# Last attention: four of twelve score tiles are clipped after the exponential, by GpSimd, and the lower bound becomes a constant

## The chip, the core and the metric

One NeuronCore of one Trainium2 chip runs the whole program as one launch. The metric is the device time of an execution in microseconds; several executions are timed and the median is given. One execution was also recorded by the hardware profiler; all rows below are from it. Engines: PE is TensorE, DVE is VectorE, ACT is ScalarE, POOL is GpSimd, SP is the queue that issues most transfers.

## The reference

Four layers, each a cross attention and a feed-forward part, on x of 32 batches x 56 tokens x 128 features, with a context of 1500 keys x 96 features for each batch. The change touches only the attention of the last layer:

```python
# B = 32, Nq = 56, Nkv = 1500, H = 16 heads of D = 8, scale = 8 ** -0.5
q = (query @ Wq + bq)      # query = layernorm(x)
k = (key_value @ Wk + bk)  # key_value = ctx_768
v = (key_value @ Wv + bv)
attn = einsum("bhqd,bhkd->bhqk", q, k) * scale
attn = clip(attn, -10000.0, 10000.0)
attn = softmax(attn, axis=-1)
attn = where(any(isnan(attn)), 1.0 / Nkv, attn)
x = x + tanh(g_xattn[3]) * (einsum("bhqk,bhkd->bhqd", attn, v) as [B, Nq, 128] @ Wo + bo)
```

## The kernel before

`clipped_pass` (line 1617) is the last attention. Each batch b has 12 key tiles of 125 keys (KT = 12, KP = 125). A score tile is 125 keys x 896, the 896 being 16 heads x 56 queries, and takes two PSUM banks of 448 columns; two such pairs (`SB`) alternate. P holds three tiles of weights in SBUF.

Keys and queries go into the tensor engine in bf16 as three parts each, and six products of parts (`NPROD`) are stacked on 96 partitions. The parts of the keys are made by `copy_keys` and `second_of_keys` on ScalarE and `rest_of_keys` (line 1846) and `third_of_keys` (line 1851) on GpSimd, three pieces of 500 columns each, and placed into the stacked tile KS by six transfers of SP (`place_keys`, line 1792). The parts of the queries are placed into QS by twelve transfers that GpSimd issues (`place_queries`, line 1769). Both run three batches ahead (b + 3), in a ring of four tiles.

The softmax needs the maximum of each row of scores before its exponentials. So each batch is scored twice. In the maximum pass 12 chunks of 112 queries x 1000 keys (`chunks`, line 1994, two matmuls) go through one pair of PSUM banks (6 and 7), and VectorE reduces each (`chunk_max`, line 2232). After the twelfth, the maximum is clipped (line 2240), GpSimd splits its negative into three bf16 parts (`max_parts`, line 1858), TensorE turns these (lines 1934 and 1935), ScalarE copies them (2128, 2129), and SP writes them as three more rows of the stacked queries, against rows of ones in the keys. The scores of the second pass thus come out with the maximum already subtracted. The same chain makes a row of lower bounds, -clip - max, which SP stores to memory and broadcasts to 125 partitions (`LB`, lines 1797 and 1801).

In the second pass each tile n goes through `score` (PE, line 2014, 8 matmuls), `clip_tile` (DVE, line 2249, from PSUM to P: min with 0, max with LB), the exponential (ACT, line 2188, in place in P), and `weigh` (PE, line 2027, 16 matmuls with the values, a column of ones giving the sum).

Every engine has its order written out by hand, in steps k = 0 to 11 of batch b. TensorE in step k: `score` of tile k + 2, `weigh` of tile k, the chunk of the maximum pass (for b + 1 if k < 3, chunks 9 to 11; else for b + 2, chunk k - 3), and at most one thing in the fifth bank (`MISC`): keys of b + 3 in k = 0, 1, 2; in k = 3 the sums of a pair of batches (even b) or the projection (odd b); the turn of the maximum of b + 1 in k = 4; the spread of the sums in k = 5 (even b); values of b + 1 in k = 7 to 10. VectorE in step k: clip of tile k + 2, maximum of that step's chunk. ScalarE before the exponential of tile n empties the fifth bank's content of step n - 3, and at n = 6, 7, 8 makes the second key parts. GpSimd in batch b: the twelve query transfers of b + 3, the key rest of piece 0, the parts of the maximum of b + 1, the rests of pieces 1 and 2, the three third parts, in even batches the norm of the pair before (lines 1882 and 1884), and in the first two batches the rows of ones (line 1743). An instruction waits for the semaphores of what it reads and of who used its buffer before; what stands behind it on its engine waits too.

Of the kernel before, what the change touches and what calls it, by code (L numbers as in the profile page):

```python
# [13 lines left out]
F32 = mybir.dt.float32  # L14
# [14 lines left out]
TT = 112  # L29
# [1556 lines left out]
class Eight(Batch):  # L1586
# [6 lines left out]

CLIP_SIGNALS = ["w_in", "q_made", "q_scaled", "q_split", "q_first", "q_zeroed", "keys_zeroed", "sums_zeroed", "ones_set",
# [5 lines left out]
                "max_in0", "max_in1", "lb_out", "lb_in0", "lb_in1", "scored", "clipped", "exped", "weighed",  # L1600
# [16 lines left out]
def clipped_pass(core, L, S, src, bo, scale, clip, csum, ctx, norm):  # L1617
# [3 lines left out]
    def sb(n, shape, dt=F32, c=ctx):  # L1621
        return core.sb(f"{L}_{n}", shape, dt, c)
# [14 lines left out]
    zero, most = sb("zero", [TT, 8]), sb("most", [TT, 8])  # L1637
    nm, r1, ST = sb("nm", [TT, 8]), sb("r1", [TT, 8]), sb("st", [TT, 32])
# [3 lines left out]
    MT, LBT = sb("mt", [24, TT], BF16), sb("lbt", [8, TT])  # L1642
    low = [nc.dram_tensor(f"{L}_low{s}", (1, HQ), F32).ap() for s in range(2)]
# [11 lines left out]
    def two(ap):  # L1655
        return ap.rearrange("p (a n) -> p a n", a=2)
# [12 lines left out]
    def chunk_of(b, k):  # L1669

        return (b + 1, 9 + k) if k < 3 else (b + 2, k - 3)

# [67 lines left out]
    def ones_in_keys(pool, n):  # L1740
        nc.gpsimd.memset(KS[n][0:96, PAIRS * NK:].bitcast(F32), 0.0).then_inc(S["keys_zeroed"], 1)
        pool.wait_ge(S["keys_zeroed"], 2 * n + 1)
        nc.gpsimd.memset(KS[n][96:128, :].bitcast(F32), TWO_ONES).then_inc(S["keys_zeroed"], 1)
        pool.wait_ge(S["keys_zeroed"], 2 * n + 2)
# [32 lines left out]
    with nc.Block() as block:  # L1777
        @block.sync
        def _(sp):
# [50 lines left out]
        def _(pool):  # L1830
            link = core.linker(pool, "pool")
            link(nc.gpsimd.memset(zero[:, :], 0.0))
            link(nc.gpsimd.memset(most[:, :], clip))
            link(nc.gpsimd.memset(ok[:, :], 0.0))

            def place_queries(b):
# [4 lines left out]
                place_products(pool, b, 0, range(NPROD), f"q_in{b.r % 4}")  # L1841
                place_products(pool, b, 1, range(0 if b.r else 3, NPROD), f"q_in{b.r % 4}")
# [11 lines left out]
            def max_parts(b):  # L1854
                done = S["parts"]

                def op(out, a, c, how):
                    nc.gpsimd.tensor_tensor(out, a, c, how).then_inc(done, 1)
                pool.wait_ge(S["max_ready"], b.lin(1, 1))
                op(nm[:, :], zero[:, :], mc[:, :], ALU.subtract)  # L1860
                op(b0[:, :], zero[:, :], mc[:, :], ALU.subtract)
                pool.wait_ge(done, b.lin(8, 2))
# [3 lines left out]
                pool.wait_ge(done, b.lin(8, 5))  # L1866
                op(b1[:, :], r1[:, :], zero[:, :], ALU.add)
                pool.wait_ge(done, b.lin(8, 6))
                op(ST[:, 8:16], b1[:, :], zero[:, :], ALU.add)
                op(ST[:, 16:24], r1[:, :], b1[:, :], ALU.subtract)  # L1870
# [45 lines left out]
        def _(pe):  # L1916
# [89 lines left out]
            def score(b, n):  # L2006
                if n == 0:
                    pe.wait_ge(S["keys_zeroed"], min(2 * b.r + 2, 8))
# [10 lines left out]
            def weigh(b, j):  # L2019
                pe.wait_ge(S["exped"], b.lin(12, j + 1))  # L2020
# [76 lines left out]
        def _(act):  # L2097
# [76 lines left out]
            def body(b):  # L2174
                for n in range(KT):
# [11 lines left out]
                    act.wait_ge(S["clipped"], b.lin(12, n + 1))  # L2187
                    nc.scalar.activation(two(P[0:KP, n % 3, :]), two(P[0:KP, n % 3, :]), ACT.Exp  # L2188
                                         ).then_inc(S["exped"], 1)
# [25 lines left out]
        def _(dve):  # L2215
# [14 lines left out]
            def chunk_max(b, c, pair=0):  # L2230
# [21 lines left out]

            def b_uses(b):
                if b.turn is None:
                    return (b.r // 2 + 1) * 16
                return 64 * b.turn + (b.r // 2 + 1) * 16
# [1521 lines left out]
```

## Time and profile before

| | |
|---|---|
| median of 3 runs | 4267.36 us (4258.15 to 4271.67) |
| profiled execution | 4270.6 us, its span 4269.0 us |
| DVE / PE / ACT / POOL busy, share of the span | 60 / 86 / 48 / 34 % |
| last attention, second passes | from 3368 to 4199 us of the span |
| transfers, mean over the span | 102 GB/s |

The profile lists each engine's busy time, groups of instructions with the idle time before them and who ended it, and instructions in order of time. "L2249" is line 2249 of the kernel. "x8" is a count, and a duration of a merged row runs from the first start to the last end. "idle before <- X" is the time that the engine stood still until X released it. Durations of matmuls include their way through the array, so neighbours overlap; differences of starts tell what a group really takes of the engine.

### The profile page before, as it was taken

The page shows a single profiled execution, that of the slowest core. Times are in us where ns is not written, and L with a number is a line of the kernel's source. Part 1 is how long each engine was busy: PE and PEld are TensorE (multiplying, and loading weights), DVE is VectorE, ACT ScalarE, POOL GpSimd, SP SyncE. Part 2 cuts the span into 40 slices and gives each one's busy share as a digit, 9 for nine tenths or more (in the row PEclk, how much of TensorE's full clock was granted, in tenths as well). Part 3 has the DMA queues.
Part 4 walks back from the last instruction along what each step waited for, and adds up shares of the span by engine and source line. Part 5 has one row for each costly group of instructions (what it writes and reads, how often), then busy time and mean ns, then how long its engine had stood idle before and what let it go on. Part 6 is the DMA issues. An engine that isn't in the chain of part 4 may idle for free. (4 is left out here: it accounts for less than half of the span.)

```text
span 4269.0 us, 84337 instructions
## 1 busy us (share of the span) xinstructions
PE 3663.6 (86%) x33162; PEld 2471.7 (58%) x33162; DVE 2581.8 (60%) x3504; ACT 2050.0 (48%) x2961; POOL 1434.1 (34%) x1893
## 2 busy tenths in 40 slices
PE   7499999936279999998999998669958799999997
PEld 7367777723146666664666666347733366666664
DVE  8556666553244455424555542457644799999995
ACT  7277777701014434442444343146522477777764
POOL 0265555122422323212322320012201666665540
PEclk9699999958669999997999998879969799999998
DMA  6277777445132323212333321011000666666650
GB/s 170 56 163 179 172 172 178 119 167 217 33 80 70 85 80 93 78 49 67 88 85 86 84 81 36 9 57 46 16 18 16 133 156 152 152 155 156 156 134 24
DMA packets 197789, 434.35 MB, mean 102 GB/s; under 512 B 46364, under 2 KB 99638, under 8 KB 197341
## 3 DMA queue, kind: packets, MB, share of 16 engines
q1 hardware_dynamic: 122636, 339.40, 30.7%
q0 software_dynamic: 39328, 47.04, 5.1%
q10 hardware_dynamic: 35504, 43.39, 3.7%
q8 instruction: 231, 3.78, 0.4%
q14 instruction: 90, 0.73, 0.1%
HBM read 244.66 MB, written 32.67 MB: 65 GB/s over the span
## 5 line engine op out<-in xcount | busy, mean ns | idle before, releaser
L1501 DVE TENSOR_REDUCE L_mp<-ps 128x2 f32<-128x1000 f32 (+1 forms) x352 | 403.3, 1151 | 555.3 <-PE ps L1320 551.9
L1483 ACT ACTIVATE L_p<-ps 125x896 f32<-125x896 f32 x384 | 352.2, 917 | 607.6 <-PE ps L1345 536.1
L1357 PE MATMUL ps<-L_p,L_cn 125*97 125x448 f32 x1536 | 639.3, 538 | 0.0
L2188 ACT ACTIVATE L_p<-L_p 125x896 f32<-125x896 f32 x384 | 364.5, 950 | 226.7 <-DVE L_p L2249 222.8
L2232 DVE TENSOR_REDUCE L_mp<-ps 112x2 f32<-112x1000 f32 x384 | 454.7, 1188 | 18.9 <-PE ps L1994 18.8
L2249 DVE SCALAR_TENSOR_TENSOR L_p<-ps,xn 125x896 f32<-125x896 f32 x384 | 413.5, 1079 | 17.1 <-PE ps L2014 16.8
L1343 PE MATMUL ps<-L_qh,L_ch 97*125 97x448 f32 x768 | 385.9, 502 | 14.5 <-DMA L_qh<-L_mc 14.5
L1357 PEld LDWEIGHTS ps<-L_p,L_cn 125*97 125x97 f32 x1536 | 250.4, 163 | 199.9 <-issue 165.9
L1994 PE MATMUL ps<-L_ks,L_qs 96*128 96x500 bf16 x768 | 236.7, 393 | 78.3 <-DVE L_mp L2232 65.5
L1344 PE MATMUL ps<-L_ql,L_ch 96*125 96x448 f32 x768 | 284.0, 370 | 0.0
L1345 PE MATMUL ps<-L_qh,L_cl 96*125 96x448 f32 x768 | 282.5, 368 | 0.0
L938 ACT ACTIVATE L_p<-ps,rk 125x896 f32<-125x896 f32 x256 | 257.6, 1007 | 51.0 <-PE ps L794 46.8
L1320 PE MATMUL ps<-L_cr,L_qb 96*128 96x500 f32 x672 | 242.8, 445 | 14.1 <-DVE L_mp L1501 8.1
L1769 POOL DMA_DIRECT2D L_qs<-L_q_part x381 | 211.9, 564 | 99.5 <-PE ps L2014 92.9
L2014 PEld LDWEIGHTS ps<-L_qs,L_ks 128*128 128x128 bf16 x3072 | 189.2, 98 | 75.0 <-issue 45.7
L794 PEld LDWEIGHTS ps<-L_qs,L_ks 128*128 128x128 bf16 x3072 | 188.1, 98 | 72.9 <-issue 54.8
L2027 PE MATMUL ps<-L_p,L_vs 125*18 125x112 f32 x6144 | 223.1, 263 | 3.4 <-ACT L_p L2188 2.9
L794 PE MATMUL ps<-L_qs,L_ks 128*128 128x112 bf16 x3072 | 216.1, 213 | 3.4 <-ACT L_p L938 3.4
L720 POOL DMA_DIRECT2D L_qs<-L_q_part x384 | 214.5, 567 | 7.6 <-DVEq L1060 6.8
L2014 PE MATMUL ps<-L_qs,L_ks 128*128 128x112 bf16 x3072 | 215.4, 213 | 1.7 <-DVE L_p L2249 1.0
L963 DVE COPY L_vs<-ps 125x384 f32<-125x384 f32 x128 | 70.9, 554 | 232.1 <-PE ps L770 232.0
L1272 POOL TENSOR_TENSOR L_un<-L_ue,L_rb 96x896 f32<-96x896 f32 x32 | 67.1, 2095 | 424.5 <-DMA L_rb<-L_den 424.5
(541 smaller groups left out, 7328.9 us busy)
## 6 DMA issues: line engine op xcount, KB each, us to landing
L_ks<-L_k_part SPq DMA_DIRECT2D x288, 375.0 KB, 6.0
L_ks<-L_k_first SPq DMA_DIRECT2D x96, 375.0 KB
moe_w<-in_L_w SPq DMA_DIRECT2D x64, 512.0 KB
L_cn<-in_ctxN SPq DMA_DIRECT2D x32, 568.4 KB
cs_ct<-in_ctxT SPq DMA_DIRECT2D x32, 562.5 KB, 4.2
L_raw<-in_ctxT SPq DMA_DIRECT2D x32, 562.5 KB, 5.0
L_cr<-in_ctxT POOLq DMA_DIRECT2D x32, 562.5 KB, 5.0
L_ch<-in_ctxT POOLq DMA_DIRECT2D x32, 562.5 KB, 4.5
```

Source lines behind the costliest of these rows:

```text
L794: mm = nc.tensor.matmul(SB[n % 2][:, m // 4, m % 4 * 2 * NQ:(m % 4 + 1) * 2 * NQ] .rearrange("p (j q) -> p j q", j=2), KS[b.r % 3][:, k0:k ...
L938: nc.scalar.activation(weights_at[n % 3][0:KP, :].rearrange("p (a n) -> p a n", a=2), SB[n % 2][0:KP], ACT.Exp, scale=rk[:, b.lin(KT, n):b ...
L1343: nc.tensor.matmul(SB[n % 2][:, a, :], CH[s][:, k], QH[s][:, q], start=True, stop=False)
L1344: nc.tensor.matmul(SB[n % 2][:, a, :], CH[s][0:DC, k], QL[s][:, q], start=False, stop=False)
L1345: mm = nc.tensor.matmul(SB[n % 2][:, a, :], CL[s][:, k], QH[s][0:DC, q], start=False, stop=True)
L1357: mm = nc.tensor.matmul(U[:, a, :], CN[s][:, j, :], P[:, n % 2, a * HALF:(a + 1) * HALF], start=(j == 0), stop=(j == KT - 1))
L1483: nc.scalar.activation(two(P[:, n % 2, :]), SB[n % 2], ACT.Exp).then_inc(S["exped"].sem, 1)
L1501: nc.vector.tensor_reduce(mp[:, 2 * k:2 * k + n], ps[:, bank:bank + n, 0:500], AX.X, ALU.max).then_inc(S["chunk_maxed"].sem, 1)
L2014: mm = nc.tensor.matmul(SB[n % 2][:, m // 4, m % 4 * 2 * NQ:(m % 4 + 1) * 2 * NQ] .rearrange("p (j q) -> p j q", j=2), KS[b.r % 4][:, k0:k ...
L2188: nc.scalar.activation(two(P[0:KP, n % 3, :]), two(P[0:KP, n % 3, :]), ACT.Exp).then_inc(S["exped"], 1)
L2232: nc.vector.tensor_reduce(mp[:, 2 * c:2 * c + 2], ps[0:TT, CB[pair], 0:500], AX.X, ALU.max).then_inc(S["chunk_maxed"], 1)
L2249: nc.vector.scalar_tensor_tensor(out=two(P[0:KP, n % 3, :]), in0=SB[n % 2][0:KP], scalar=0.0, in1=two(LB[0:KP, b.r % 2, :]), op0=ALU.min, ...
```

## The change

Tiles 2, 6, 8 and 11 of each batch (`FLOORED`) are no longer clipped by VectorE. ScalarE takes their exponential straight from PSUM into P, and GpSimd then bounds the weights in P in place, min with 1 and max with exp(-64). Their PSUM pair is free when the exponential is done, their weights are ready when GpSimd is done. The other eight tiles are clipped by VectorE with two constants, 0 and -64, in place of the row. The row of lower bounds, its subtraction, transpose, copy, store and broadcast are gone; the maximum is clipped to [64 - clip, clip]. The order of GpSimd changes: the four bounds stand among its other work, and the twelve query transfers are spread in three groups of four. The rows of ones are filled in halves.

```diff
+RANGE = 64.0
+LEAST = float(np.exp(-RANGE))
+    FLOORED = (2, 6, 8, 11)
+    CLIPPED = [n for n in range(KT) if n not in FLOORED]
+    def bank_read(b, n):
+        if n in FLOORED:
+            return S["exped"], b.lin(12, n + 1)
+        return S["clipped"], b.lin(8, CLIPPED.index(n) + 1)
+    def weights_ready(b, n):
+        if n in FLOORED:
+            return S["floored"], b.lin(4, FLOORED.index(n) + 1)
+        return S["exped"], b.lin(12, n + 1)
...
             def place_max(b):
                 sp.wait_ge(S["turn_copied"], b.lin(1, 1))
-                sp.dma_start(low[b.r % 2].rearrange("o (t n) -> (o t) n", t=8), LBT[:, :]).then_inc(S["lb_out"], 16)
                 sp.dma_start(QS[b.r % 4][96:99, 0:HQ].rearrange("r (m n) -> r m n", n=2 * NQ), MT[:, :]
                              ).then_inc(S[f"max_in{b.r % 2}"], 16)
-                sp.wait_ge(S["lb_out"], b.lin(16, 16))
-                sp.dma_start(LB[0:KP, b.r % 2, :], low[b.r % 2].to_broadcast([KP, HQ])
-                             ).then_inc(S[f"lb_in{b.r % 2}"], 16)
...
-                op(ST[:, 24:32], nm[:, :], most[:, :], ALU.subtract)
...
+            def floor_tile(b, n):
+                pool.wait_ge(S["exped"], b.lin(12, n + 1))
+                nc.gpsimd.tensor_scalar(P[0:KP, n % 3, :], P[0:KP, n % 3, :], 1.0, LEAST, ALU.min, ALU.max
+                                        ).then_inc(S["floored"], 1)
+
             def body(b):
-                if (b + 3).there():
-                    place_queries(b + 3)
-                if (b + 3).there():
+                keys = (b + 3).there()
+                floor_tile(b, 2)
+                if keys:
+                    place_queries(b + 3, range(0, 2))
                     rest_of_keys(b + 3, 0)
                 if (b + 1).there():
                     max_parts(b + 1)
-                if (b + 3).there():
-                    for c in (1, 2):
-                        rest_of_keys(b + 3, c)
-                    for c in range(3):
-                        third_of_keys(b + 3, c)
+                if keys:
+                    rest_of_keys(b + 3, 1)
+                floor_tile(b, 6)
+                if keys:
+                    rest_of_keys(b + 3, 2)
+                    third_of_keys(b + 3, 0)
+                floor_tile(b, 8)
+                if keys:
+                    third_of_keys(b + 3, 1)
+                    third_of_keys(b + 3, 2)
+                    place_queries(b + 3, range(2, 4))
+                if b.r < 2:
+                    nc.gpsimd.memset(KS[b.r + 2][0:96, PAIRS * NK:].bitcast(F32), 0.0).then_inc(S["keys_zeroed"], 1)
+                    pool.wait_ge(S["keys_zeroed"], 3 * (b.r + 2) + 1)
+                    ones_row_part(pool, b.r + 2, 0)
+                floor_tile(b, 11)
                 if b.r % 2 == 0 and (b - 2).there():
                     norm(b - 2)
+                if keys:
+                    place_queries(b + 3, range(4, NPROD))
                 if b.r < 2:
-                    pool.wait_ge(S["keys_third"], (b + 3).lin(3, 3))
-                    ones_in_keys(pool, b.r + 2)
+                    pool.wait_ge(S["floored"], b.lin(4, 4))
+                    ones_row_part(pool, b.r + 2, 1)
...
             def turn(b):
-                pe.wait_ge(S["parts"], b.lin(8, 8))
-                nc.tensor.transpose(ps[0:24, 5, 0:TT], ST[:, 0:24], core.ident[0:TT, 0:TT])
-                nc.tensor.transpose(ps[0:8, 5, 128:128 + TT], ST[:, 24:32], core.ident[0:TT, 0:TT]
-                                    ).then_inc(S["turned"], 1)
+                pe.wait_ge(S["parts"], b.lin(7, 7))
+                nc.tensor.transpose(ps[0:24, 5, 0:TT], ST[:, 0:24], core.ident[0:TT, 0:TT]).then_inc(S["turned"], 1)
...
-                if b.turn is not None or b.r or n >= 2:
-                    pe.wait_ge(S["clipped"], b.lin(12, n - 1))
+                if n >= 2:
+                    pe.wait_ge(*bank_read(b, n - 2))
+                elif b.r:
+                    pe.wait_ge(*bank_read(b - 1, n + KT - 2))
...
             def weigh(b, j):
-                pe.wait_ge(S["exped"], b.lin(12, j + 1))
+                pe.wait_ge(*weights_ready(b, j))
...
-                nc.scalar.activation(LBT[:, :], ps[0:8, 5, 128:128 + TT], ACT.Copy)
...
+                    if n in FLOORED:
+                        act.wait_ge(S["scored"], b.lin(12, n + 1))
+                        if b.r or n >= 3:
+                            act.wait_ge(S["weighed"], b.lin(12, n - 2))
+                        nc.scalar.activation(two(P[0:KP, n % 3, :]), SB[n % 2][0:KP], ACT.Exp
+                                             ).then_inc(S["exped"], 1)
...
-                nc.vector.tensor_scalar(mc[:, :], mu[:, :], clip, -clip, ALU.min, ALU.max
+                nc.vector.tensor_scalar(mc[:, :], mu[:, :], clip, RANGE - clip, ALU.min, ALU.max
                                         ).then_inc(S["max_ready"], 1)
 
             def clip_tile(b, n):
-                if n == 0:
-                    dve.wait_ge(S[f"lb_in{b.r % 2}"], b_uses(b))
+                if n in FLOORED:
+                    return
                 dve.wait_ge(S["scored"], b.lin(12, n + 1))
                 if b.turn is not None or b.r or n >= 3:
                     dve.wait_ge(S["weighed"], b.lin(12, n - 2))
-                nc.vector.scalar_tensor_tensor(out=two(P[0:KP, n % 3, :]), in0=SB[n % 2][0:KP], scalar=0.0,
-                                               in1=two(LB[0:KP, b.r % 2, :]), op0=ALU.min, op1=ALU.max
-                                               ).then_inc(S["clipped"], 1)
+                nc.vector.tensor_scalar(two(P[0:KP, n % 3, :]), SB[n % 2][0:KP], 0.0, -RANGE, ALU.min, ALU.max
+                                        ).then_inc(S["clipped"], 1)
```

## Rows read from the trace of the kernel before

**Rows 1.** Table of stretches, four steady batches: busy time of each engine, clock, DMA share, GB/s.
```profile
3576.00:3680.00 104.00, 95.70 (x1404) 64.14 (x1406) 102.44 (x106) 74.10 (x118) 62.85 (x108) 1.00 0.69 156
```

**Rows 2.** Groups by line, same stretch: busy us, mean ns, idle before and releaser.
```profile
L2232 DVE TENSOR_REDUCE L_mp<-ps 112x2 f32<-112x1000 f32 x48 | 57.1, 1189 | 0.0
L2249 DVE SCALAR_TENSOR_TENSOR L_p<-ps,xn 125x896 f32<-125x896 f32 x48 | 51.8, 1079 | 1.3 <-PE ps L2014 1.3
...
L1769 POOL DMA_DIRECT2D L_qs<-L_q_part x48 | 26.7, 564 | 14.3 <-PE ps L2014 14.3
...
L1846 POOL TENSOR_TENSOR L_k_full<-L_k_full,L_k_first 128x500 f32<-128x500 f32 x12 | 13.5, 1141 | 9.9 <-ACT L_k_full L2112 9.9
```

**Rows 3.** Waits, same stretch: us in total, times, longest.
```profile
PEld ps L1994 <- DVE L_mp L2232: 16.2, 37, 0.9
...
DVE L_p L2249 <- PE ps L2014: 1.3, 4, 0.3
```

**Rows 4.** Order of time, one values step: start us, length us, engine, line.
```profile
3660.70 0.60 PE L1994 MATMUL ps<-L_ks,L_qs 96*128 96x500 bf16 x2
3661.14 0.82 PE L1927 MATMUL ps<-L_wve,L_cv 97*125 97x128 f32 x6
3661.56 1.19 DVE L2232 TENSOR_REDUCE L_mp<-ps 112x2 f32<-112x1000 f32 x1
...
3661.79 0.56 PE L2014 MATMUL ps<-L_qs,L_ks 128*128 128x112 bf16 x8
3662.28 0.58 PE L2027 MATMUL ps<-L_p,L_vs 125*18 125x112 f32 x16
...
3662.81 0.60 PE L1994 MATMUL ps<-L_ks,L_qs 96*128 96x500 bf16 x2
```

**Rows 5.** Order of time, odd batch: chunk matmuls and one key projection.
```profile
3669.12 0.60 PE L1994 MATMUL ps<-L_ks,L_qs 96*128 96x500 bf16 x2 [0.60 <-DVE L_mp L2232]
...
3671.39 0.60 PE L1994 MATMUL ps<-L_ks,L_qs 96*128 96x500 bf16 x2
...
3672.05 1.11 PE L1920 MATMUL ps<-L_ck,L_wk 97*128 97x500 f32 x2
...
3673.99 0.60 PE L1994 MATMUL ps<-L_ks,L_qs 96*128 96x500 bf16 x2
...
3676.27 0.60 PE L1994 MATMUL ps<-L_ks,L_qs 96*128 96x500 bf16 x2
...
3678.65 0.60 PE L1994 MATMUL ps<-L_ks,L_qs 96*128 96x500 bf16 x2
...
3680.54 0.60 PE L1994 MATMUL ps<-L_ks,L_qs 96*128 96x500 bf16 x2 [0.20 <-DVE L_mp L2232]
```

**Rows 6.** Order of time, even batch: chunk matmuls around step 4.
```profile
3652.18 0.60 PE L1994 MATMUL ps<-L_ks,L_qs 96*128 96x500 bf16 x2 [0.19 <-DVE L_mp L2232]
...
3654.39 0.60 PE L1994 MATMUL ps<-L_ks,L_qs 96*128 96x500 bf16 x2 [0.52 <-DVE L_mp L2232]
```

**Rows 7.** Groups by line and shape, whole run.
```profile
L1483 ACT ACTIVATE L_p<-ps 125x896 f32<-125x896 f32 x384 | 352.2, 917 | 607.6 <-PE ps L1345 536.1 <-PE ps L1357 71.5
...
L1263 POOL TENSOR_TENSOR L_ql<-L_qp,L_qh 96x896 fp32r<-96x896 f32 x32 | 67.1, 2096 | 0.0
...
L1247 POOL CAST L_qb<-L_qp 96x896 fp32r x20 | 37.0, 1852 | 0.0
...
L1257 POOL CAST L_qh<-L_qp 96x896 fp32r x20 | 18.9, 944 | 0.0
```

**Rows 8.** Order of time, even batch, ScalarE: exp of tile 6.
```profile
3653.45 0.93 ACT L2188 ACTIVATE L_p<-L_p 125x896 f32<-125x896 f32 x1
```

**Rows 9.** Order of time, SP queue: first key transfers of an even batch.
```profile
3658.54 1.22 SPq L1792 DMA_DIRECT2D L_ks<-L_k_first  x2
```

**Rows 10.** Table of stretches, one microsecond, columns as in group 1.
```profile
3674.00:3675.00 1.00, 1.00 (x8) 0.51 (x5) 1.00 (x2) 0.55 (x2) 0.00 (x0) 1.00 0.14 23
```

**Rows 11.** Transfers into the query tiles, same stretch as group 1.
```profile
DMA to landing us min/median/max: 5.7/7.1/8.2
```

More of the change, by code:

```diff
@@ L1599 @@
                 "chunk_scored", "chunk_maxed", "max_found", "max_ready", "parts", "turned", "turn_copied",
-                "max_in0", "max_in1", "lb_out", "lb_in0", "lb_in1", "scored", "clipped", "exped", "weighed",
+                "max_in0", "max_in1", "scored", "clipped", "floored", "exped", "weighed",
                 "u_copied", "sums_picked", "sums_widened", "sums_spread", "sums_copied", "sums_inverted", "u_normed", "seen", "projected", "out_copied"]
@@ L1636, in clipped_pass @@
     mp, mu, mc = sb("mp", [TT, 24]), sb("mu", [TT, 8]), sb("mc", [TT, 8])
-    zero, most = sb("zero", [TT, 8]), sb("most", [TT, 8])
-    nm, r1, ST = sb("nm", [TT, 8]), sb("r1", [TT, 8]), sb("st", [TT, 32])
+    zero = sb("zero", [TT, 8])
+    nm, r1, ST = sb("nm", [TT, 8]), sb("r1", [TT, 8]), sb("st", [TT, 24])
     b0, b1 = sb("b0", [TT, 8], BF16), sb("b1", [TT, 8], BF16)
@@ L1641, in clipped_pass @@
     ok, row_ok, row_bad, bad = sb("ok", [128, 2 * QV]), sb("row_ok", [128, 1]), sb("row_bad", [128, 1]), sb("bad", [128, 1], I32)
-    MT, LBT = sb("mt", [24, TT], BF16), sb("lbt", [8, TT])
-    low = [nc.dram_tensor(f"{L}_low{s}", (1, HQ), F32).ap() for s in range(2)]
+    MT = sb("mt", [24, TT], BF16)
     SB = [ps[:, 0:2, 0:HALF], ps[:, 2:4, 0:HALF]]
@@ L1741, in ones_in_keys, with ones_row_part @@
         nc.gpsimd.memset(KS[n][0:96, PAIRS * NK:].bitcast(F32), 0.0).then_inc(S["keys_zeroed"], 1)
-        pool.wait_ge(S["keys_zeroed"], 2 * n + 1)
-        nc.gpsimd.memset(KS[n][96:128, :].bitcast(F32), TWO_ONES).then_inc(S["keys_zeroed"], 1)
-        pool.wait_ge(S["keys_zeroed"], 2 * n + 2)
+        pool.wait_ge(S["keys_zeroed"], 3 * n + 1)
+        for c in range(2):
+            ones_row_part(pool, n, c)
+    def ones_row_part(pool, n, c):
+        w = (PAIRS * NK + 4) // 2
+        nc.gpsimd.memset(KS[n][96:128, c * w:(c + 1) * w].bitcast(F32), TWO_ONES).then_inc(S["keys_zeroed"], 1)
+        pool.wait_ge(S["keys_zeroed"], 3 * n + 2 + c)
     def loads(sp):
@@ L1832, in _, with place_queries @@
             link(nc.gpsimd.memset(zero[:, :], 0.0))
-            link(nc.gpsimd.memset(most[:, :], clip))
             link(nc.gpsimd.memset(ok[:, :], 0.0))
-            def place_queries(b):
+            def place_queries(b, products=range(NPROD)):
                 pool.wait_ge(S["q_split"], b.r // 8 + 1)
@@ L1840, in place_queries @@
                     pool.wait_ge(S["scored"], b.lin(12, -36))
-                place_products(pool, b, 0, range(NPROD), f"q_in{b.r % 4}")
-                place_products(pool, b, 1, range(0 if b.r else 3, NPROD), f"q_in{b.r % 4}")
+                for j in range(2):
+                    place_products(pool, b, j, [u for u in products if b.r or j == 0 or u >= 3], f"q_in{b.r % 4}")
             def rest_of_keys(b, c):
@@ L1861, in max_parts @@
                 op(b0[:, :], zero[:, :], mc[:, :], ALU.subtract)
-                pool.wait_ge(done, b.lin(8, 2))
+                pool.wait_ge(done, b.lin(7, 2))
                 op(r1[:, :], nm[:, :], b0[:, :], ALU.subtract)
                 op(ST[:, 0:8], b0[:, :], zero[:, :], ALU.add)
-                op(ST[:, 24:32], nm[:, :], most[:, :], ALU.subtract)
-                pool.wait_ge(done, b.lin(8, 5))
+                pool.wait_ge(done, b.lin(7, 4))
                 op(b1[:, :], r1[:, :], zero[:, :], ALU.add)
-                pool.wait_ge(done, b.lin(8, 6))
+                pool.wait_ge(done, b.lin(7, 5))
                 op(ST[:, 8:16], b1[:, :], zero[:, :], ALU.add)
@@ L2007, in score @@
                 if n == 0:
-                    pe.wait_ge(S["keys_zeroed"], min(2 * b.r + 2, 8))
+                    pe.wait_ge(S["keys_zeroed"], min(3 * b.r + 3, 12))
                     pe.wait_ge(S[f"max_in{b.r % 2}"], uses(b, 2, 16))
-                if b.turn is not None or b.r or n >= 2:
-                    pe.wait_ge(S["clipped"], b.lin(12, n - 1))
+                if n >= 2:
+                    pe.wait_ge(*bank_read(b, n - 2))
+                elif b.r:
+                    pe.wait_ge(*bank_read(b - 1, n + KT - 2))
                 for m in range(PAIRS):
@@ L2186, in body @@
                             second_of_keys(b + 3, c)
-                    act.wait_ge(S["clipped"], b.lin(12, n + 1))
-                    nc.scalar.activation(two(P[0:KP, n % 3, :]), two(P[0:KP, n % 3, :]), ACT.Exp
-                                         ).then_inc(S["exped"], 1)
+                    if n in FLOORED:
[4 more added lines that the diff above has]
+                                             ).then_inc(S["exped"], 1)
+                    else:
+                        act.wait_ge(S["clipped"], b.lin(8, CLIPPED.index(n) + 1))
+                        nc.scalar.activation(two(P[0:KP, n % 3, :]), two(P[0:KP, n % 3, :]), ACT.Exp
+                                             ).then_inc(S["exped"], 1)
             def split_keys(b):
@@ L2248, in clip_tile @@
                     dve.wait_ge(S["weighed"], b.lin(12, n - 2))
-                nc.vector.scalar_tensor_tensor(out=two(P[0:KP, n % 3, :]), in0=SB[n % 2][0:KP], scalar=0.0,
-                                               in1=two(LB[0:KP, b.r % 2, :]), op0=ALU.min, op1=ALU.max
-                                               ).then_inc(S["clipped"], 1)
[L2253 to L2256, printed above, removed]
+                nc.vector.tensor_scalar(two(P[0:KP, n % 3, :]), SB[n % 2][0:KP], 0.0, -RANGE, ALU.min, ALU.max
+                                        ).then_inc(S["clipped"], 1)
             def invert(b):
```

## The prediction

> **What bounds the kernel now.** Read the table of stretches first. The last attention's steady part runs from about 3395 to 4175 us, and in four whole batches of it VectorE is busy 102.4 of 104 us, TensorE 95.7, ScalarE 74.1, GpSimd 62.9, at the full granted clock of 1.00 (2.4 GHz) [rows 1]. So VectorE looks like the bound. The groups by line say what fills it: per batch twelve score maxima of 1.189 us and twelve clips of 1.079 us [rows 2]. The waits say how near the next engine is: VectorE waits 1.3 us in 104, while TensorE's weight loads for the next chunk of the maximum pass wait 16.2 us for the maximum before [rows 3]. That pass has one pair of PSUM banks, so chunk, maximum, next chunk is a chain of its own, whatever the clips do.
>
> Then lay the steps of a batch side by side, measuring from one chunk matmul (line 1994) to the next. In a step with values the pitch is 3662.81 - 3660.70 = 2.11 us [rows 4], and TensorE is filled by it: chunk 0.44, values 0.65, scores 0.49, weighing 0.53 (differences of the starts in [rows 4]), sum 2.11. VectorE's clip and maximum, 2.27 by their durations, overlap at the seams and fill the same 2.1, since it hardly ever idles. In the three steps with keys the pitch is 2.27, 2.60 and 2.28 and TensorE is the bound; the 2.60 holds a wait of TensorE for ScalarE's copy of the keys before [rows 5]. In the step after, odd batches project (3678.65 - 3676.27 = 2.38, TensorE [rows 5]); the even ones' next step takes 2.21 [rows 6], the odd ones' 1.89 [rows 5]. All steps together are 26.2 us a batch.
>
> **Part 1, four clips leave VectorE.** 4 x 1.079 = 4.3 us a batch by durations, 138 over 32 batches. Little of it is on the path. Without its clip a step falls not to the maximum alone but to the larger of two things. One is the chunk chain: 0.60 for the chunk [rows 4], 0.06 to the reader (taken as long as the gap behind it), 1.19 for the maximum, 0.06 back (3661.56 + 1.19 to 3662.81 [rows 4]), which is 1.91. The other is TensorE's own work. Skipped tiles 2, 6, 8, 11 are clipped in steps k = 0, 4, 6, 9.
> - k = 0 (keys): TensorE needs 2.27, saves 0.
> - k = 4: even 2.21 to 1.91, saves 0.30; odd is at 1.89 already, 0.
> - k = 6 (no extra matmul): 2.10 to 1.91, saves 0.19.
> - k = 9 (values): TensorE needs 2.11, saves 0. VectorE is then ahead by some 0.2, and in the free step k = 11 about 0.10 comes back.
> Even 0.59, odd 0.29.
>
> The eight clips that stay become a two-scalar instruction with PSUM as its one tensor. No row has that form at this size, so I bound it from both sides by its neighbours that read PSUM: the old clip, 1.079 for the same 896 columns, and the maximum scaled to them, 1.189 x 896/1000 = 1.065 [rows 2]. I take 1.08, no change; the other end would be 8 x 0.014 = 0.1 us a batch, and only in steps that VectorE bounds.
>
> **Part 2, exp straight from PSUM.** ScalarE's exp from PSUM of the same shape costs 0.917 in another attention [rows 7], against 0.93 from SBUF here [rows 8]: nothing. What counts is order. Exp 2 no longer waits for a clip, so it runs about 1.1 us earlier (the length of that clip), and the first key copy behind it, which now ends just before TensorE's 3672.05 [rows 5], too. The stall in the 2.60 step, 2.60 - 2.28 = 0.32, goes. But exp 3 still follows a clip, so the second key copy hardly moves and is late next: between 0 and 0.32 is kept, I take 0.17. The score banks of floored tiles are freed by exp, whose start is a ScalarE slot; it falls before the score that needs it by about 0.5 us, nothing.
>
> **Part 3, Pool's four bounds.** The instruction is in the profile nowhere. Below: a one-input cast of 96x896, 0.94; above: the two-input subtraction of the same columns, 2.10, with another cast at 1.85 between [rows 7]. The bound has one input and one output of four bytes and no second tensor, so it is nearest to 0.94; I take 0.95, and keep 0.9 to 2.1. Pool's load goes from 15.7 (62.9/4) to 15.7 - 0.2 + 3.8 = 19.3 of 26 us: it fits, but in order. Each floored tile's weights are ready 0.95 + 0.1 after its exp. Tile 6 in even batches has the least room, since ScalarE does the widening and a key part before its exp, so that exp stays where it was: it ends at 3654.4 [rows 8]. The bound then ends at 3655.4 at 0.95. The weighing of tile 6 stands before chunk 6, which comes at 3654.39 + 2.10 = 3656.5 [rows 6], less the 0.30 saved, less its own 0.53: 3655.7. Cost at 0.95: nothing, 0.3 to spare; above about 1.2 the excess is paid in even batches.
>
> The Trainium skill (GPSIMD Engine Reference, "Elementwise — side-by-side cycle accounting") gives a body of at most two operations 1.03 cycles an element, and 1.8 for a tight loop. At its 1.2 GHz 896 elements are 0.77 us by the one and 1.34 by the other, before dispatch, an estimate from the page. The trace's casts, 0.94 and 1.85 [rows 7], lie about the two; which speed the bound gets, no row shows.
>
> **Part 4, what moves on Pool and SP.** The third key parts now stand behind bounds 6 and 8, and bound 8 waits for its exp. They end at 3658.5 in the even batch (SP issues the key transfers then [rows 9]); new, 2 x 0.95 for the bounds, and 1.1 of waiting for exp 8, because the third key subtraction (1.14 [rows 2]), which ScalarE's part of the keys ahead of exp 8 needs, now comes after bound 6: 3.0 later, 3661.5. The DMA share drops at 3674 [rows 10], so keys and the values' load behind them are down by then; the keys are needed at step k = 3 of the next batch, 3676.27 [rows 5]. 3.0 later without the 437 KB row of bounds in front, they land about a microsecond before the new need (3676.27 less the 0.8 saved = 3675.5). The queries are nearer. Twelve issues of 0.564 [rows 2] stood ahead of everything; now the last four follow: 3661.5 + 4 x 0.564 + bound 11 at 0.95 + in even batches the norm, 2 x 1.14 (as other Pool subtractions of 500 columns [rows 2]) + 4 x 0.564 = 3669.2. The last starts at 3668.7 and lands 5.7 to 8.2 later, median 7.1 [rows 11]: 3674.4 to 3676.9, 3675.8 by the median, 0.3 late for even batches. Odd ones, without the norm, have 2.0 to spare. Cost 0.3 in every other batch, 0.15 a batch (0 to 0.7).
>
> Removed: one transpose of 0.1 on TensorE, one ScalarE copy, one Pool subtraction of 0.2, the store and the broadcast on SP. All beside other work: turning waits for nothing, the bounds' row was loaded eight steps ahead. Their cover gone, they would be 0.4 us a batch; as a gain I take 0. The memset of ones in halves touches the first two batches only, and the prologue's wait for keys may shrink by up to 1 us with fewer query transfers beside it; 0 taken, -5 to +3 kept.
>
> **The sum.** Mean of even and odd: 0.44 (Part 1) + 0.17 - 0.15 = 0.46 us a batch; 30 full batches: 13.8 us. The profiled execution took 4270.6 (span 4269.0 and 1.6 around it), so 4256.8; it lies 3.2 above the median of 4267.4, so against the median 4253.6, say 4254. What then ends last in most steps is TensorE or the one-pair chunk chain.
>
> **Rivals.**
> - R1, Pool is slow or late. If the bound takes about 1.85 (the slow cast [rows 7]), three of them stand before the last query transfer: 2.7 later, 3.0 late in even batches and 0.7 in odd, mean 1.85 against 0.61 won: +1.24 x 30 = 37 slower, 4304. It decides from about 1.1 us for the bound. For it: in-order Pool with DMA issues between, and no row of this operation. Against it: the 0.94 cast. By the 1.8 cycles of the Trainium skill's page (1.5 us with dispatch, an estimate from it) the even batches would be 1.95 late, +0.37 x 30 = 11 slower, 4278, inside this rival.
> - R2, bound near 0.95 but the transfers land at 8.2: even 1.4 late, 0.7 a batch, which eats the 0.61: 4270, no change. For it: the DMA share is over 0.9 whenever they travel. Against it: the row of bounds is gone from the queue.
> - R3, everything comes through: key stall 0.32, no late transfer, -0.76 x 31 = 24 and 4 of prologue: 4240. For it: TensorE's busy time allows no more than that.
>
> **How the numbers follow.** Forecast 0.50, R1 0.23, R2 0.15, R3 0.12. About 12.8 us (0.3%) is what a measurement here tells from no change, and the forecast's 13.8 lies on that edge: its own range is 4242 to 4264, and it goes 0.28 to faster and 0.22 to same; R3 to faster; R2 0.13 to same and 0.02 to slower, R1 to slower. Faster 0.40, same 0.35, slower 0.25. Range 4238 to 4290: it reaches R3 and about half of R1.
>
> **What would show it.** Chunk pitch 1.9 in steps 4 (even) and 6, unchanged 2.1 in the values' steps, no more wait of line 1920 for the key copy in step 1; Pool's bound at 0.95; line 1994 waiting for a query transfer once in two batches at k = 3, by under 1 us; VectorE busy near 85% of the stage. Batch 25.7 instead of 26.2. It is wrong if Pool's bound is over 1.1, if TensorE waits for it anywhere, or if steps with values get shorter.

## The result

| | median | range | ratio to before, 95% interval |
|---|---|---|---|
| before | 4265.0 us | 4258.15 to 4271.67 | |
| after | 4304.5 us | 4301.93 to 4306.31 | 1.0092 [1.0075, 1.011] |

The change costs 39.5 us where 13 less were forecast. 4304 is the time that R1 gave, but the cause is not R1's: GpSimd's bound is as fast as forecast. The profiled execution took 4306.31 us, its span is 4304.5 us, 35.5 more than before. The last chunk matmul starts 33.6 us later than before (4203.9 against 4170.3), so the loss lies in the last attention.

First the same views as before, of the changed kernel. The table of stretches, four batches (busy time of PE, PEld, DVE, ACT, POOL, granted clock, DMA share, GB/s), answers to [rows 1]:
```profile
3603.00:3707.00 104.00, 92.19 (x1331) 63.08 (x1329) 83.81 (x84) 67.99 (x109) 74.16 (x112) 0.97 0.60 126
```
VectorE fell from 102.4 to 83.8 of 104 us, but TensorE fell too, from 95.7 to 92.2: less work was done in the same time, and the clock is no longer 1.00 throughout. Nothing is full. The groups by line of that stretch answer to [rows 2] and [rows 7]:
```profile
L2272 DVE TENSOR_REDUCE L_mp<-ps 112x2 f32<-112x1000 f32 x46 | 55.0, 1195 | 19.8 <-PE ps L2026 19.7
L2289 DVE TENSOR_SCALAR L_p<-ps 125x896 f32<-125x896 f32 x30 | 32.5, 1084 | 0.2
...
L1790 POOL DMA_DIRECT2D L_qs<-L_q_part x44 | 25.0, 573 | 0.3
...
L1903 POOL TENSOR_SCALAR L_p<-L_p 125x896 f32<-125x896 f32 x16 | 14.9, 932 | 23.4 <-ACT L_p L2224 23.2
L2224 ACT ACTIVATE L_p<-ps 125x896 f32<-125x896 f32 x16 | 14.5, 904 | 0.0
```
Here is what the operations that the change brings cost: the bound 0.932 us, the exp from PSUM 0.904, the two-scalar clip 1.084. All three are as forecast. And the waits of that stretch (us in total, times, longest), which answer to [rows 3]:
```profile
PEld ps L2026 <- DVE L_mp L2272: 13.0, 34, 0.9
PEld ps L2026 <- issue: 8.3, 10, 4.2
...
PE ps L2026 <- issue: 6.3, 2, 4.0
```
The telling row is the last one: the chunk matmul stood still twice, for 6.3 us together, and no engine is named. "Issue" is idle time whose releaser the profile does not show; a transfer can hide there. In order of time, TensorE's chunk matmuls around one of the two kinds of place (start, length, idle before):
```profile
3954.52 0.60 PE L2026 MATMUL ps<-L_ks,L_qs 96*128 96x500 bf16 x2
3956.80 0.60 PE L2026 MATMUL ps<-L_ks,L_qs 96*128 96x500 bf16 x2
3961.72 0.98 PE L2026 MATMUL ps<-L_ks,L_qs 96*128 96x500 bf16 x2 [2.52 <-issue]
3965.61 0.60 PE L2026 MATMUL ps<-L_ks,L_qs 96*128 96x500 bf16 x2
```
The steps are 2.28, then 4.92, then 3.89; in the repaired kernels below the same three are 2.28, 2.34 and 2.31. The chunk at 3961.72 is the first one that reads the queries of a new batch (k = 3). GpSimd before it:
```profile
3947.53 0.93 POOL L1903 TENSOR_SCALAR L_p<-L_p 125x896 f32<-125x896 f32 x1
3948.55 1.14 POOL L1897 TENSOR_TENSOR L_ok<-L_ok,L_rd 128x448 f32<-128x448 f32 x1
3949.64 1.14 POOL L1899 TENSOR_TENSOR L_un<-L_ue,L_rd 128x448 f32<-128x448 f32 x1
3950.72 2.29 POOL L1790 DMA_DIRECT2D L_qs<-L_q_part  x4
```
The last of the twelve query transfers starts at 3950.72 + 3 x 0.57 = 3952.43. The next two fences are the landing lines of two such last groups, the four transfers from 3950.72 and the four of another pair of batches, from 3619.18:
```profile
DMA to landing us min/median/max: 6.7/7.8/9.2
```
```profile
DMA to landing us min/median/max: 6.5/7.8/10.6
```
3952.43 + 9.2 = 3961.6, and the chunk restarts at 3961.72. In the other pair 3619.18 + 3 x 0.58 + 10.6 = 3631.5, and the chunk restarts at 3631.64 after 3.97 us of standing still. The fourth transfer is the slowest in both groups. One wait of this kind, that of the last pair of batches, has its releaser in the profile by name:
```profile
4179.83 0.65 PE L2026 MATMUL ps<-L_ks,L_qs 96*128 96x500 bf16 x2 [3.88 <-DMA L_qs<-L_q_part]
```
And it is so throughout: in all 14 pairs from 3430 to 4204 the fourth transfer of this group lands after 7.7 to 11.1 us, and the chunk restarts 0.03 to 0.25 us behind its landing. In one of them, the pair of 51.9 us, the fourth lands after 7.7 us, at 3576.66, and the wait goes on for another moment, for the keys:
```profile
3576.91 0.60 PE L2026 MATMUL ps<-L_ks,L_qs 96*128 96x500 bf16 x2 [1.23 <-DMA L_ks<-L_k_part]
```
SP's queue (start, length) and the stretches around the wait say what else travels and what the wait brings with it:
```profile
3949.02 1.72 SPq L1813 DMA_DIRECT2D L_ks<-L_k_first  x1
3950.79 0.66 SPq L1813 DMA_DIRECT2D L_ks<-L_k_part  x1
3951.49 0.99 SPq L1754 DMA_DIRECT2D L_cv<-in_ctxT  x1
```
```profile
3950.00:3954.00 4.00, 3.65 (x54) 2.09 (x46) 3.31 (x4) 2.66 (x5) 3.67 (x6) 1.00 1.03 209
...
3958.00:3962.00 4.00, 1.48 (x26) 0.85 (x25) 1.98 (x4) 2.37 (x4) 2.37 (x8) 0.97 1.04 209
3962.00:3964.00 2.00, 2.00 (x10) 1.83 (x9) 1.20 (x1) 0.00 (x0) 0.00 (x0) 0.50 0.47 111
3964.00:3966.00 2.00, 2.00 (x28) 1.42 (x28) 0.00 (x0) 1.57 (x3) 0.00 (x0) 0.71 0.00 0
```
The key transfers of 375 KB and the 562 KB of the values' context go out in the same microseconds, and the DMA engines are full (share 1.03). After the wait TensorE's granted clock is 0.50 (its 1.2 GHz level) for two microseconds and 0.71 in the mean of the next two, in which it comes back to 1.00, with TensorE busy all of the time: so the step behind the wait takes 3.89 for about 2.3. This pair of batches thus pays 2.6 for the wait and 1.6 for the clock. A pair took 52.37 us before (24 chunk steps, the same to 0.01 in 13 pairs); now it takes 51.9 to 57.3.

### The profile page after: what moved, and what is told of

The parts are those of the page before. It is cut to its first block and busy times, and to the rows that moved or that the text cites. A ratio compares the mean times of both kernels' runs of the same rounds, so it can differ in the third digit from the quotient of the medians.

```text
span 4304.5 us, 84207 instructions
## 1 busy us (share of the span) xinstructions
PE 3677.1 (85%) x33130; PEld 2485.3 (58%) x33130; DVE 2472.7 (57%) x3376; ACT 2032.9 (47%) x2929; POOL 1551.0 (36%) x1992
## 5 line engine op out<-in xcount | busy, mean ns | idle before, releaser
L2228 ACT ACTIVATE L_p<-L_p 125x896 f32<-125x896 f32 x256 | 243.2, 950 | 182.6 <-DVE L_p L2289 182.0
L2289 DVE TENSOR_SCALAR L_p<-ps 125x896 f32<-125x896 f32 x256 | 277.7, 1085 | 17.0 <-PE ps L2048 14.8
L710 POOL TENSOR_TENSOR L_k_part<-L_k_rest,L_k_part 128x500 bf16<-128x500 f32 x96 | 109.0, 1138 | 299.0 <-ACT L_k_part L903 298.9
```

The costliest lines, as they stand in the source:

```text
L2289: nc.vector.tensor_scalar(two(P[0:KP, n % 3, :]), SB[n % 2][0:KP], 0.0, -RANGE, ALU.min, ALU.max).then_inc(S["clipped"], 1)
```

## The experiments

**What is in question.** Theory T: the last query transfers of a batch come too late, because GpSimd starts them late and they land slowly, and everything else in the change is a gain. Rivals: the two other uses of GpSimd (the norm, the parts of the keys), ScalarE or PSUM with the exp from PSUM, or the constants themselves. A time below is followed by its ratio to the kernel before, timed on the same chip, with the 95% interval.

**Queries by SP.** All twelve transfers of a batch leave GpSimd and stand at the head of SP's body; the four bounds stay.
```diff
+            def sp_queries(b):
+                if b.r >= 4:
+                    sp.wait_ge(S["scored"], b.lin(12, -36))
+                for j in range(2):
+                    place_products(sp, b, j, range(NPROD), f"q_sp{b.r % 4}")
...
-                    place_queries(b + 3, range(0, 2))
...
-                    place_queries(b + 3, range(2, 4))
...
-                    place_queries(b + 3, range(4, NPROD))
```


> The changed kernel, with the twelve query transfers of each batch issued by SP at the head of its batch instead of by GpSimd in three groups. Theory Q (the last query transfers land late for step 3 of every odd batch; 4.9 and 3.9 us where 2.28 and 2.38 were, 4.1 us a pair of batches): the stall goes, 15 pairs x 4.1 = 62 us less than 4304, so about 4243, chunk pitch 2.3 in step 2. Theory K (the key transfers land late, because the third key parts are made 3 us later): GpSimd issues 2.3 us less ahead of them only in part, keys start at most 1 us earlier, and most of the stall stays: 4285 to 4300.

Measured: 4244.28 us, 0.9948 [0.9931, 0.9964]; a pair 50.56 to 51.16 us, the waits of 2.5 us and more and the low clock behind them gone. The change with this one move is faster than before: the transfers are the loss, the way through ACT, PSUM and GpSimd is not. What is left of a wait, up to 0.6 us in the step before k = 3 of odd batches (2.94 for 2.34), is for the keys, by name:
```profile
3459.82 0.60 PE L2033 MATMUL ps<-L_ks,L_qs 96*128 96x500 bf16 x2 [0.52 <-DMA L_ks<-L_k_part]
```

**The norm behind the last queries.** The two norm operations of even batches (2.2 us) change places with the last query group.
```diff
-                if b.r % 2 == 0 and (b - 2).there():
-                    norm(b - 2)
                 if keys:
                     place_queries(b + 3, range(4, NPROD))
+                if b.r % 2 == 0 and (b - 2).there():
+                    norm(b - 2)
```


> The changed kernel, with GpSimd's norm behind the last group of query transfers instead of ahead of it; key transfers are not touched. Theory Q: the last group starts 2.3 us earlier in even batches, the 2.6 us stall shrinks to about 0.3 and the clock stays up: 4245 to 4260. Theory K: unchanged, 4304, or a little slower because the sums' buffer comes free 2.3 us later (ScalarE waits 0.9 us for it now).

Measured: 4291.52 us, 1.0055 [1.0039, 1.0072], 13 better than the change, and 30 short of what Theory Q gave: a pair still takes about 54.1. The wait has moved. In order of time, all engines:
```profile
3726.31 0.60 PE L2026 MATMUL ps<-L_ks,L_qs 96*128 96x500 bf16 x2
...
3727.89 1.13 POOL L1899 TENSOR_TENSOR L_un<-L_ue,L_rd 128x448 f32<-128x448 f32 x1
3729.12 0.36 ACT L2168 ACTIVATE L_ue<-ps 128x224 f32<-128x224 f32 x1 [3.17 <-POOL L_un L1899]
...
3730.09 1.01 PE L2026 MATMUL ps<-L_ks,L_qs 96*128 96x500 bf16 x2
```
ScalarE's copy of the next pair's sums overwrites what the late norm still reads (3.17 us of waiting), the exp behind it is late, and TensorE's step takes 3.78; the clock fell again (0.53 from 3730 to 3732) and the next step took 3.88. In these steps no query was waited for. So the norm had no room either, and its place ahead of the queries was paid for.

**Without the last query group.** In the steady loop the last four query transfers of every batch (products 4 and 5) are left out.
```diff
-                if keys:
-                    place_queries(b + 3, range(4, NPROD))
```


> The changed kernel without the last group of four query transfers of each batch from batch 3 on (the products of the third parts are left out of the scores). Theory Q: no wait at step 3 of odd batches, about 4240. Theory K: the wait stays within 0.5 us of what it is, above 4295.

Measured: one run, 4252.56 us; a pair 50.6 to 52.1, 51.04 in the mean of 13. Step 2 of odd batches takes 2.3 to 3.7 us for 2.34, and the profile names the keys there:
```profile
3820.07 0.60 PE L2025 MATMUL ps<-L_ks,L_qs 96*128 96x500 bf16 x2 [1.24 <-DMA L_ks<-L_k_part]
```
So Theory K holds too, for a small part: the keys are up to 1.3 us late, which costs about 0.5 us a pair once the queries do not hide it. The other 3.9 of the 4.4 us that a pair loses hang on four transfers of 7 KB.

**Keys in parts.** GpSimd is left as in the change; only SP's order is. The three transfers of the first key parts go as soon as these are there, the other three later, instead of all six in one burst.
```diff
+                if (b + 3).there():
+                    place_keys_early(b + 3, 0)
                 if (b + 1).there():
                     place_max(b + 1)
                 if (b + 3).there():
-                    place_keys(b + 3)
+                    place_keys_early(b + 3, 1)
+                    place_keys_early(b + 3, 2)
```


> The changed kernel, with SP placing the first parts of the keys (three of six transfers) as soon as they are made, and the others behind the maximum's rows; the query transfers are where they were. Theory K: keys land 5 us earlier, the stall goes: 4240 to 4250. Theory Q: the last query group is issued at the same time and still lands 7 to 10 us later; the stall stays unless the emptier rings bring it down earlier: 4285 to 4304.

Measured: 4248.07 us, 0.9953 [0.9936, 0.9969]; every pair but the first and last ones 50.57 us. GpSimd (the last query group, behind the norm), SP, the chunk that needs the queries, the landing of the four transfers from 3659.66, and the stretch in which they travel:
```profile
3659.66 2.29 POOL L1790 DMA_DIRECT2D L_qs<-L_q_part  x4
```
```profile
3642.77 2.32 SPq L1805 DMA_DIRECT2D L_ks<-L_k_first  x3
...
3650.10 4.69 SPq L1805 DMA_DIRECT2D L_ks<-L_k_part  x3
```
```profile
3668.06 0.60 PE L2034 MATMUL ps<-L_ks,L_qs 96*128 96x500 bf16 x2
```
```profile
DMA to landing us min/median/max: 2.3/2.9/3.2
```
```profile
3659.00:3665.00 6.00, 5.65 (x80) 3.13 (x69) 5.27 (x6) 4.29 (x7) 5.61 (x10) 1.00 0.42 105
```
This is the run that separates the two halves of T. GpSimd issues as late as in the change: the fourth transfer starts at 3659.66 + 3 x 0.58 = 3661.40, 6.66 us before its need at 3668.06, where the change has 6.65. But it lands after 3.2 us (2.1 to 3.5 over all these groups) in place of 7.7 to 11.1, because the key burst has been issued and moved before. The lateness of the issue alone does not cost anything: a late issue and a full set of DMA engines together do. The time, 4248, is the one that Theory K gave; this run moves keys and queries at once and could not tell one from the other, which the two runs with the keys untouched (queries by SP, no last group) do. By the Trainium skill (DMA: Bandwidth & Descriptors, "Anatomy of one DMA — SWDGE (gpsimd) path") a transfer takes 2.0 us and its bytes at 436 GB/s, 2.0 for 7 KB, an estimate from the page; the trace is near it where the engines are nearly free (1.7 us for the four from 3637.70 of this run, with a DMA share of 0.06) and three to five times it where they are not.

**Constants alone, then GpSimd's new order alone.** The first kernel is the one before with the two constants and without the row of bounds, no tile by GpSimd, and the old order. The second adds the new order of GpSimd, still without any bound.
```diff
-    FLOORED = (2, 6, 8, 11)
+    FLOORED = ()
```


> The kernel before with the constant bounds alone: all twelve clips stay on VectorE as min with 0, max with -64, the row of bounds is gone, GpSimd's order is that of before. Theory (the row was hidden): 4264 to 4268, clip 1.08 us, pair of batches 52.4. Rival (its 437 KB broadcast held up transfers or its wait held up the clips): 4255 or less.

> The same with GpSimd's new order too (queries in three groups, the last behind the norm), but no floored tile. Theory Q with the bounds as the cause of the delay: the last query group starts 3 x 0.93 + 1.1 = 3.9 us earlier against the step that needs it than in the changed kernel (6.65 ahead there, so 10.5), more than the 9 to 11 us landing only just; pair 52.4 to 52.8, 4264 to 4272. If the order alone is at fault: the stall of 2.6 plus 1.5 at low clock a pair appears here too, 4320.

Measured: constants alone 4265.0 us, 0.9993 [0.9984, 1.0003], a pair 52.37; with the new order 4265.11 us, 0.9995 [0.9986, 1.0005], a pair 52.36. Taking away the row, its transpose, store and 437 KB broadcast is worth nothing, as forecast. In the second kernel the last query group is issued in the same place of GpSimd's order; GpSimd and the chunk matmuls (a landing line for the four from 3812.11 behind them):
```profile
3812.11 4.47 POOL L1790 DMA_DIRECT2D L_qs<-L_q_part  x8
```
```profile
3823.24 0.60 PE L2022 MATMUL ps<-L_ks,L_qs 96*128 96x500 bf16 x2
3825.52 0.60 PE L2022 MATMUL ps<-L_ks,L_qs 96*128 96x500 bf16 x2
```
```profile
DMA to landing us min/median/max: 6.0/7.5/8.6
```
The fourth starts at 3813.8, is down at 3822.4 at the latest, and is needed at 3825.52: a lead of 11.7 us, and 3 to spare. So the order as such is harmless where GpSimd has this time left. The lead of the change is 3956.80 + 2.28 - 3952.43 = 6.65.

**GpSimd's time alone.** The second kernel of the last section with five operations a batch on a scratch tile that nobody reads, where the bounds would be.
```diff
+            def idle_tile():
+                link(nc.gpsimd.tensor_scalar(idle[0:KP, :], idle[0:KP, :], 1.0, LEAST, ALU.min, ALU.max))
```


> The kernel is f2_pool_order_alone (no tile is bounded in SBUF, Pool's order as in the changed kernel) with five operations added on GpSimd that nobody reads: the same tensor_scalar on a scratch tile, at the places in Pool's order where the changed kernel has its bounds ahead of the last group of query transfers. Theory Q (Pool's time ahead of the last queries is what makes them late): the lead of the last transfer falls from 11.7 us by about 4.7 (five times 0.93) to about 7, as in the changed kernel, its landing takes 9 to 11 us, one chunk step of each pair of batches waits 2 to 3 us and the next runs at the lower clock: about 4 us a pair over 52.36, 15 pairs, so about 4265 + 60 = 4325 us. Rival (the way through ACT and SBUF itself, the exp from PSUM or the wait for the bound, is needed for the loss): no wait, pair 52.36, 4265 us.

Measured: 4297.21 us, 1.008 [1.006, 1.01]. GpSimd, the chunk matmuls and one stretch behind the wait:
```profile
3672.13 0.93 POOL L1904 TENSOR_SCALAR L_idle<-L_idle 125x896 f32<-125x896 f32 x1
...
3675.34 4.50 POOL L1791 DMA_DIRECT2D L_qs<-L_q_part  x8
```
```profile
3682.43 0.60 PE L2032 MATMUL ps<-L_ks,L_qs 96*128 96x500 bf16 x2
3687.71 0.99 PE L2032 MATMUL ps<-L_ks,L_qs 96*128 96x500 bf16 x2 [2.94 <-issue]
3691.58 0.60 PE L2032 MATMUL ps<-L_ks,L_qs 96*128 96x500 bf16 x2
```
```profile
3689.00:3691.00 2.00, 2.00 (x15) 1.85 (x14) 0.94 (x1) 0.58 (x2) 1.53 (x2) 0.50 0.00 0
```
The fourth transfer starts at 3675.34 + 3 x 0.56 = 3677.02, lands after 10.6, and 3687.71 is the restart: in this pair the whole pattern of the change, steps of 5.28 and 3.87, the clock at 0.50, with no tile going through ACT and SBUF. So the rival that needs that way falls. The size was half of what was expected: 2.4 us a pair (54.8 against 52.36), not 4. The lead is 7.7, one us more; two pairs have hardly a wait; and in six of the others the slow step does not follow, not even behind waits of 2.76 and 2.95 us, where the next steps are 2.30 and 2.29.

**Two tiles of four.** Queries by SP, and only tiles 6 and 8 bounded by GpSimd.
```diff
-    FLOORED = (2, 6, 8, 11)
+    FLOORED = (6, 8)
```


> Queries issued by SP, but only tiles 6 and 8 floored (VectorE skips its clip in steps 4 and 6). By steps: 0.32 in even batches and 0.20 in every batch, 0.72 a pair of batches, pair 51.65; the 2.60 step stays 2.60, step 11 stays 2.10: 4252 to 4258. If the time went with VectorE's busy time it would be half of the gain of all four tiles, the same 4255; the steps tell them apart.

Measured: 4257.34 us, 0.9965 [0.9951, 0.9979]; a pair 51.62. The keys' steps of this kernel, the wait in its own view:
```profile
4103.14 0.60 PE L2031 MATMUL ps<-L_ks,L_qs 96*128 96x500 bf16 x2
4105.73 0.60 PE L2031 MATMUL ps<-L_ks,L_qs 96*128 96x500 bf16 x2
4108.01 0.60 PE L2031 MATMUL ps<-L_ks,L_qs 96*128 96x500 bf16 x2
```
```profile
PEld ps L1956 <- ACT L_k_full L2151: 3.0, 8, 0.5
```
The step of 2.59 is back, with its wait for ScalarE's key copy, and it is 2.28 wherever tile 2 goes straight from PSUM. So tiles 6 and 8 have no part in removing the stall of [rows 5]. That tile 2 does it and not tile 11 is argued from the order, in which the key copy stands right behind exp 2; no run has the one without the other. Tiles 6 and 8 are worth 0.75 of the 1.80 us a pair, 2 and 11 the rest.

**Both repairs.** Queries by SP and keys in parts, all four tiles.

> Floored tiles with both cures: queries issued by SP, keys placed in parts. Each alone left a pair of batches at 50.6 to 50.9, so nothing more is to win in the steady part: 50.57 a pair, 4240 to 4246. If late keys cost the first cure its scatter (pairs up to 51.1), this one is at 50.57 throughout, 3 us below it.

Measured: 4241.11 us (4238.21 to 4243.81), 0.9931 [0.9914, 0.9947]; a pair 50.55 in every pair between the first and the last. The same four batches:
```profile
3603.00:3707.00 104.00, 97.92 (x1460) 66.37 (x1459) 92.21 (x94) 74.35 (x120) 53.17 (x74) 1.00 0.60 142
```
TensorE 97.9 of 104 at the full clock. This is the version to keep: it beats both kernels, the one after by 63 us.

**A fifth tile.** The kernel just told, with tile 7 too.
```diff
-    FLOORED = (2, 6, 8, 11)
+    FLOORED = (2, 6, 7, 8, 11)
```


> The kernel is f3_sp_queries_keys_in_parts with score tile 7 given to ACT and Pool too (five of twelve: 2, 6, 7, 8, 11). By the steps as measured in the versions free of the query wait (a clip taken out of DVE's chain is worth what its step exceeds TensorE's own work): about 0.2 us a batch, pair 50.15 instead of 50.55, about 4235 us against 4241. Rival (ACT or Pool becomes the bound with a fifth tile: three neighbouring tiles bounded one after the other on Pool, each waited for by its weighing): a wait of up to 1 us a batch, pair 51 to 52.5, 4250 to 4270 us.

Measured: 4264.62 us, 0.9999 [0.999, 1.0009]; a pair 51.87 in most and 53.4 in four of them, so 23 us are given back. In order of time:
```profile
4069.44 0.93 POOL L1919 TENSOR_SCALAR L_p<-L_p 125x896 f32<-125x896 f32 x1 [1.74 <-ACT L_p L2240]
...
4071.55 1.13 POOL L1883 TENSOR_TENSOR L_k_part<-L_k_full,L_k_part 128x500 bf16<-128x500 f32 x1
...
4072.77 1.94 POOL L1919 TENSOR_SCALAR L_p<-L_p 125x896 f32<-125x896 f32 x2
4073.75 0.58 PE L2077 MATMUL ps<-L_p,L_vs 125*18 125x112 f32 x16 [1.77 <-POOL L_p L1919]
```
The bound of tile 7 stands behind two key subtractions and starts at 4072.77, and the weighing of tile 7 waits 1.77 us for it: my rule of the steps missed it, the rival had it. A step of 3.27 comes once a pair, and in the first of the four long pairs the clock is seen to fall behind it (0.50 from 3603 to 3605). The rule holds only while the bound is ready before its weighing. Whether tile 7 pays with its bound ahead of the subtractions was not tried.

## Why the prediction was wrong

The step that failed is Part 4's last line, "The last starts at 3668.7 and lands 5.7 to 8.2 later, median 7.1: ... 0.3 late for even batches". The start was right: the lead over the need is 6.65 us where the working gives 6.8. The landing was not: 9.2 and 10.6 us for the transfer that decides in the two groups shown, 7.7 to 11.1 over all, and the 8.2 of [rows 11] was no upper bound. Two faults are in it. I took the median of the twelve transfers of a batch for a wait that the slowest of the last four ends; and I took the landing of the old place for that of the new one. The old place was not free of the burst either: in the trace before the twelve start at 3662.93, behind the first keys of [rows 9], the DMA share is 1.03 from 3660, and they land after 6.6 to 8.2, the twelfth after 7.4. R2 had the mechanism, with 8.2 for the price. R2 named the DMA share of over 0.9 and drew about one microsecond from it; "keys in parts" shows that the burst is the cause of the slow landing, since it goes to 2.1 to 3.5 with GpSimd untouched.

The same Part has the keys "about a microsecond before the new need". Their issue was forecast well (14.0 us before the need, measured 13.8), but they too land late, by up to 1.3 us, as the run without the last query group shows; mostly that is hidden behind the queries.

The second miss is a term that is not in the sum at all: what a wait of two to four microseconds of TensorE does to its clock. In seven of the 13 steady pairs it adds 1.5 to 1.6 us to the next step, in one 1.4, in three (the longest waits) 1.9 and up to 0.4 more in the step after, and in two nothing. The short waits of "queries by SP", up to 0.6 us, have no such price. So a pair lost 4.4 us where 0.3 were reckoned.

The accounts, per pair of batches, the change against before: predicted 2 x (0.44 + 0.17) = 1.22 won and 0.30 lost. Measured 1.80 won (52.37 to 50.57, in "keys in parts") and 4.4 lost (50.57 to 54.97, the mean of the 13 steady pairs). 13 x 2.60 = 33.8 us, and the last whole pair adds 54.06 - 51.22 = 2.8; the span grew by 35.5, the rest being the first batches and the end.

- Part 1. Step 4 in even batches 2.21 to 1.89 (0.30 said, 0.32 measured), step 6 2.10 to 1.90 (0.19 and 0.20), step 9 nothing, step 11 2.11 to 1.92 (0.10 and 0.19). Right, the last at half of what it was. Step 3, which is not in the sum, gives 0.06 more. VectorE's clips at 1.084: right.
- Part 2. The stall of 0.32 goes wholly (2.60 to 2.28), and 0.06 of it comes back in the next step (2.28 to 2.34): 0.26 is won where 0.17 was taken. Exp from PSUM costs nothing: right.
- Part 3. The bound takes 0.932 (0.95 said), and nothing waits for it between 3435 and 4204 (the first and the last batch have waits of 3.7 us in all): R1's mechanism is false. By the two rates of the Trainium skill (GPSIMD Engine Reference, "Elementwise — side-by-side cycle accounting") 896 elements were 0.77 and 1.34 us before dispatch, an estimate from the page: the trace has 0.93, below the second, so it fits the lower rate alone. The five-tile run shows how near it is all the same: one bound more, behind other work, and TensorE waits 1.77.
- The removed row of bounds: nothing, right (constants alone). The order as such: nothing (order alone). Keys by SP in time: not quite, see above.
- R3, "everything comes through", said 4240; with both repairs the time is 4241.11. Its gain a batch was low (0.76, measured 0.90), so part of the agreement is luck. The change was sound and its transfers were not.

R1's time, 4304, was hit by chance: its mechanism did not happen, and another one of the same size did.

Open: why the fourth transfer takes 8.5 to 11.1 us in the burst while the first of its group takes 6.2 to 6.9 and the twelve of the trace before, in a burst as full, 6.6 to 8.2; why it takes only 7.7 in the pair of 51.9 us; and why the clock falls behind some waits and not behind others as long. The runs change when the burst comes, not what it is made of.

## What to carry to other kernels

When work is added to an engine that also issues transfers, write down for the last transfer behind it the lead over its need, and take for its landing the worst row of a stretch in which the DMA engines are as full as they will be at the new place, and not the median. Here the worst row, 8.2, against a lead of 6.8 would have given the sign, though not the size: the transfer took 7.7 to 11.1. If the lead is short, moving the big transfers apart is as good as moving the small ones forward (4248 and 4244 us), and either turned the same change from 0.9% slower to 0.5% faster. And price a TensorE wait of two microseconds or more with the slow step that can stand behind it, not by its length alone.

## What was not expected of the hardware

- A 7 KB transfer issued by GpSimd landed after 1.7 us with the DMA engines nearly free (share 0.06, "keys in parts") and after 5.8 to 11.1, in the last groups of even batches, with their share at 1.0. The fourth of such a group was the slowest or as slow as the third in all 14.
- After TensorE had stood still for 1.83 to 4.4 us the granted clock fell to 0.50 in 11 of 13 steady pairs, and the next step took 3.7 to 4.2 us for 2.31; in the pair with the wait of 3.97 it was still 0.50 from 3635 to 3637, with the restart at 3631.64. But behind waits of 2.28 us (this kernel) and 2.76 and 2.95 (GpSimd's time alone) it stayed at 1.00, and the next steps took 2.29 to 2.30. The length of the wait alone does not decide it.
- A clip from PSUM with two constants (1.084 us) costs what the clip with a second tensor from SBUF did (1.079).
